# Attention block on one core: projection weights laid out contraction index first by the host

## What is computed

```
x = x + _L0_cond_ref(x, ...); x = x + _L1_cond_ref(x, ...); x = x + _L2_cond_ref(x, ...)
q = jnp.einsum('bsd,ed->bse', x, Wq).reshape(bsz, seqlen, HQ, D)      # 32 heads of 128
k = jnp.einsum('bsd,ed->bse', x, Wk).reshape(bsz, seqlen, HK, D)      # 8 heads of 128
v = jnp.einsum('bsd,ed->bse', x, Wv).reshape(bsz, seqlen, HK, D)
q = _rope(_rmsnorm(q, q_norm_w), pos); k = _rope(_rmsnorm(k, k_norm_w), pos)
...                                                                   # paged cache of keys and values, softmax
return jnp.einsum('bse,de->bsd', o.reshape(bsz, seqlen, HQ * D), Wo)
```

## Time and profile before

| | us |
|---|---|
| median of 3 runs (2461.73 to 2463.17) | 2462.31 |
| the profiled execution | 2460.18 |
| its span, first to last instruction | 2458.0 |
| PE busy | 2359.9 (96%) |
| DVE busy | 1774.6 (72%) |
| ACT busy | 1348.4 (55%) |
| POOL busy | 1152.9 (47%) |
| mean granted TensorE clock, share of full | 0.982 |

### The profile page before, as it was taken

The page is one execution under the profiler, slowest core; times in us unless marked ns, Lnnn a source line. Parts: engine busy times, 40 slices in busy tenths (PEclk is TensorE's granted clock), DMA queues, the critical chain, the costliest instruction groups (busy, mean ns, idle before and its releaser), DMA issues. The chain is left out here.

```text
span 2458.0 us, 51373 instructions
## 1 busy us (share of the span) xinstructions
PE 2359.9 (96%) x15297; PEld 1973.4 (80%) x15297; DVE 1774.6 (72%) x3412; ACT 1348.4 (55%) x2635; POOL 1152.9 (47%) x1362
## 2 busy tenths in 40 slices
PE   6988899999999499999999999999999997999999
PEld 5337777777777399999999999999999997888887
DVE  4656288988889588888888888888888886432221
ACT  6653387788777355555555555555555554321111
POOL 0322134443444277767777777777776774000000
PEclk9999999999999699999999999999999999999999
DMA  9335323333232588888888888888888885743442
GB/s 315 98 102 180 90 80 93 108 108 103 90 107 86 171 274 297 293 292 276 295 288 296 279 287 297 292 289 278 292 295 297 272 293 183 211 126 99 133 137 60
DMA packets 470906, 501.43 MB, mean 204 GB/s; under 512 B 102069, under 2 KB 396981, under 8 KB 466742
## 3 DMA queue, kind: packets, MB, share of 16 engines
q1 hardware_dynamic: 433974, 366.37, 47.2%
q0 software_dynamic: 36864, 134.23, 15.6%
HBM read 404.02 MB, written 96.47 MB: 204 GB/s over the span
## 5 line engine op out<-in xcount | busy, mean ns | idle before, releaser
L1134 POOL TENSOR_TENSOR att_probs<-att_probs,att_inverse 128x512 f32<-128x512 f32 x512 | 536.0, 1047 | 288.6 <-DVE att_inverse L1330 284.0
L1238 ACT ACTIVATE att_probs<-att_probs,att_low 128x544 f32<-128x544 f32 x512 | 383.7, 750 | 515.3 <-DVE att_low L1317 452.0
L1195 PE MATMUL att_o<-att_probs_t,att_values 128*128 128x128 f32 x4096 | 540.9, 275 | 0.0
L1317 DVE CUSTOM_DVE_ANT_0 att_probs<-att_score,att_mask,att_batch_cols 128x544 f32<-128x544 f32 x512 | 400.0, 781 | 138.6 <-PE att_score L1160 99.9
L1195 PEld LDWEIGHTS att_o<-att_probs_t,att_values 128*128 128x128 f32 x4096 | 497.6, 192 | 0.0
L1326 DVE COPY att_probs_t<-att_turn 128x512 f32<-128x512 f32 x512 | 350.7, 685 | 1.2 <-PE att_turn L1175 1.2
L1120 POOL DMA_INDIRECT att_values<-L_cond_v_cache,att_v_rows_of x256 | 282.1, 1102 | 83.1 <-POOL att_v_rows_of L1116 48.8
L1160 PE MATMUL att_score<-att_keys_raw,att_queries_raw 128*128 128x288 f32 (+1 forms) x1024 | 290.7, 407 | 29.5 <-DMA att_queries_raw<-q_t 27.3
L1175 PE MATMUL att_turn<-ident,att_probs 128*128 128x128 f32 x2048 | 311.0, 274 | 1.2 <-POOL att_probs L1134 0.8
L1293 DVE TENSOR_TENSOR att_keys_lo<-att_keys_raw,att_keys_hi 128x384 fp32r<-128x384 f32 (+1 forms) x320 | 259.3, 811 | 17.6 <-ACT att_keys_hi L1231 17.6
L1175 PEld LDWEIGHTS att_turn<-ident,att_probs 128*128 128x128 f32 x2048 | 244.1, 141 | 33.3 <-POOL att_probs L1134 1.4
(11 more groups left out here) (140 smaller groups left out, 4103.1 us busy)
## 6 DMA issues: line engine op xcount, KB each, us to landing
att_keys_raw<-L_cond_k_cache SPq DMA_DIRECT2D x1024, 128.0 KB
q_t<-proj_q_out SPq DMA_DIRECT2D x32, 1024.0 KB, 3.9
att_queries_raw<-q_t SPq DMA_DIRECT2D x64, 512.0 KB
o_t<-att_heads_out SPq DMA_DIRECT2D x64, 512.0 KB, 6.6
out_o_raw<-o_t SPq DMA_DIRECT2D x32, 1024.0 KB, 5.7
prep_natural<-L_cond_weight SPq DMA_DIRECT2D x16, 1024.0 KB, 8.0
w_nat<-L_cond_Wq SPq DMA_DIRECT2D x8, 1024.0 KB, 5.8
v_new<-values_v_out SPq DMA_DIRECT2D x64, 128.0 KB, 2.1
```

What stands on the lines that cost most here:

```text
L1134: nc.gpsimd.tensor_tensor(probs[:, k, 0:L], probs[:, k, 0:L], inverse[:, k:k + 1].to_broadcast([P, L]), ALU.mult).then_inc(probs_ready, 1)
L1195: last = nc.tensor.matmul(o, values[j][:, t, h * D:(h + 1) * D], probs_t[m % 2][:, t * P:(t + 1) * P], start=(t == 0), stop=False, skip_gr ...
L1238: nc.scalar.activation(probs[:, k, :], probs[:, k, :], ACT.Exp, bias=low[k][:, 0:1], scale=-1.0, accum_out=total[k][:, 0:1]).then_inc(exp_ ...
L1317: nc.vector.tensor_tensor_reduce(out=probs[:, k, :], in0=score_ps[:, LEFT:LEFT + KEYS], in1=mask[j][:], scale=batch_cols[j][:, h:h + 1], s ...
```

## The change

The host hands Wv, Wk, Wq and Wo over with the contracted index first (it is not part of the timed program), so a load puts the contracted index on the partitions at once. The transposes of weights go from all three stages. ScalarE and VectorE read the loaded rows in SBUF where they read a bank in PSUM. The waits for `w_turned` become waits for `w_ready` (both halves taken), and ScalarE waits for the load itself. In `projection` the two banks of `proj_w` are gone and `RING` goes from 4 to 5.

```
@@ load_wv
-    sp.dma_start(tile[:], wv.rearrange("(h p) i -> p h i", p=P)[:, heads]).then_inc(loaded, 16)
+    sp.dma_start(tile[:], wv.rearrange("p h c e -> p h (c e)")[:, heads]).then_inc(loaded, 16)
@@ stage_values
+        def wv_rows(h):
+            return w_nat[:, h] if h < WV_EARLY else wv_nat[:, h - WV_EARLY]
...
-            sp.wait_ge(w_turned, WV_EARLY)
+            sp.wait_ge(w_ready, WV_EARLY)
...
-            for h in range(HK):
-                if h == WV_EARLY:
-                    pe.wait_ge(wv_loaded, 16)
-                rows = w_nat[:, h] if h < WV_EARLY else wv_nat[:, h - WV_EARLY]
-                if h >= BANKS:
-                    pe.wait_ge(w_ready, h - BANKS + 1)
-                for c in range(IC):
-                    last = nc.tensor.transpose(w_ps[h % BANKS][:, c * P:(c + 1) * P], rows[:, c * P:(c + 1) * P], ident[:])
-                last.then_inc(w_turned, 1)
             pe.wait_ge(w_ready, HK)
...
             def split_weights(h):
-                act.wait_ge(w_turned, h + 1)
-                nc.scalar.activation(wvt_hi[:, :, h * D:(h + 1) * D], w_ps[h % BANKS].rearrange("p (c e) -> p c e", c=IC),
+                if h == WV_EARLY:
+                    act.wait_ge(wv_loaded, 16)
+                nc.scalar.activation(wvt_hi[:, :, h * D:(h + 1) * D], wv_rows(h).rearrange("p (c e) -> p c e", c=IC),
                                      ACT.Copy).then_inc(wv_hi_ready, 1)
...
-                nc.vector.tensor_tensor(wvt_lo[:, :, cols], w_ps[h % BANKS].rearrange("p (c e) -> p c e", c=IC),
+                nc.vector.tensor_tensor(wvt_lo[:, :, cols], wv_rows(h).rearrange("p (c e) -> p c e", c=IC),
@@ stage_projection
-        RING = 4
+        RING = 5
...
-                    if rc == 1 and not last_head:
-                        turn_weights(h + 1, 1 - u, m)
-
-            for m in range(M):
-                turn_weights(0, 0, m, True)
...
-                act.wait_ge(w_turned, h * M + (m + 1))
-                nc.scalar.activation(w_hi[u][:, m].rearrange("p c e -> p (c e)"), w_ps[(u * M + m) % 2][:],
+                if m == 0 and not first:
+                    act.wait_ge(w_loaded, h * 32)
+                nc.scalar.activation(w_hi[u][:, m].rearrange("p c e -> p (c e)"), w_nat[:, m, :],
...
-                nc.vector.tensor_tensor(w_lo[u][:, m].rearrange("p c e -> p (c e)"), w_ps[(u * M + m) % 2][:],
+                nc.vector.tensor_tensor(w_lo[u][:, m].rearrange("p c e -> p (c e)"), w_nat[:, m, :],
@@ stage_output
-                sp.dma_start(wo_nat[v][:], wo.rearrange("(c p) e -> p c e", p=P)[:, :, h * (REP * D):(h + 1) * (REP * D)]
+                sp.dma_start(wo_raw[v][:], wo[bass.ds(h, 1)].rearrange("h p r o -> p (h r) o")).then_inc(wo_loaded[v], 16)
...
-                sp.wait_ge(turned, (h - 1) * REP)
+                sp.wait_ge(w_ready, (h - 1) * REP)
...
-            turn_weights(0)
             for h in range(HK):
-                if h < HK - 1:
-                    turn_weights(h + 1)
                 pe.wait_ge(w_ready, (h + 1) * REP)
                 products(0, h, True)
@@ LAYOUTS, applied by the host
+    "L3_cond_Wv": lambda a: a.reshape(HK, D, IC, P).transpose(3, 0, 2, 1),
+    "L3_cond_Wk": lambda a: a.reshape(HK, D, IC, P).transpose(0, 3, 2, 1),
+    "L3_cond_Wq": lambda a: a.reshape(HK, REP, D, IC, P).transpose(0, 4, 1, 3, 2),
+    "L3_cond_Wo": lambda a: a.reshape(HID, HK, REP, D).transpose(1, 3, 2, 0),
```

More of the change, by code:

```diff
@@ L469, in stage_values @@
     GC = G // RC
-    BANKS = 4
     with ExitStack() as ctx:
@@ L491, in stage_values @@
         row_f = a_.sb("row_f", [P, 1])
-        w_ps = [a_.ps(f"w{n}") for n in range(BANKS)]
         v_ps = [a_.ps(f"v{u}{n}") for u in range(U) for n in range(2)]
@@ L698, in load_head_weights @@
 def load_head_weights(sp, wq, wk, w_nat, h, loaded):
-    sp.dma_start(w_nat[:, 0, :], wk[bass.ds(h * D, D)]).then_inc(loaded, 16)
-    sp.dma_start(w_nat[:, 1:, :], wq[bass.ds(h * (REP * D), REP * D)].rearrange("(m p) i -> p m i", p=P)).then_inc(loaded, 16)
+    sp.dma_start(w_nat[:, 0, :], wk[bass.ds(h, 1)].rearrange("h p c e -> p (h c e)")).then_inc(loaded, 16)
+    sp.dma_start(w_nat[:, 1:, :], wq[bass.ds(h, 1)].rearrange("h p m c e -> p (h m) (c e)")).then_inc(loaded, 16)
 def stage_projection(nc, wq, wk, ident, x3t_hi, x3t_lo, rope, w_nat, stat, qt_dram, kn_dram):
@@ L727, in stage_projection @@
         stat_t = a_.sb("stat_t", [P, CB, S])
-        w_ps = [a_.ps(f"w{n}") for n in range(2)]
         proj_ps = [a_.ps(f"proj{k}") for k in range(RING)]
@@ L769, in head @@
                 if not last:
-                    sp.wait_ge(w_turned, M)
-                    sp.wait_ge(w_turned, h * M + M)
+                    sp.wait_ge(w_ready, M)
+                    sp.wait_ge(w_ready, h * M + M)
                     load_head_weights(sp, wq, wk, w_nat, h + 1, w_loaded)
@@ L787, in _ @@
         def _(pe):
-            def turn_weights(h, u, m, first=False):
-                if m == 0 and not first:
-                    pe.wait_ge(w_loaded, h * 32)
-                n = (u * M + m) % 2
-                if m >= 2 or not first:
-                    pe.wait_ge(w_ready, h * M + (m - 1))
-                for c in range(IC):
-                    last = nc.tensor.transpose(w_ps[n][:, c * P:(c + 1) * P], w_nat[:, m, c * P:(c + 1) * P], ident[:])
-                last.then_inc(w_turned, 1)
             def sum_k(h, rc):
@@ L843, in _, with split_weights @@
         def _(act):
-            def split_weights(h, u, m):
-                act.wait_ge(w_turned, h * M + (m + 1))
-                nc.scalar.activation(w_hi[u][:, m].rearrange("p c e -> p (c e)"), w_ps[(u * M + m) % 2][:],
+            def split_weights(h, u, m, first=False):
+                if m == 0 and not first:
+                    act.wait_ge(w_loaded, h * 32)
+                nc.scalar.activation(w_hi[u][:, m].rearrange("p c e -> p (c e)"), w_nat[:, m, :],
                                      ACT.Copy).then_inc(w_hi_ready, 1)
@@ L878, in _ @@
             for m in range(M):
-                split_weights(0, 0, m)
+                split_weights(0, 0, m, True)
             heads(act, head)
@@ L1374, in stage_output @@
         a_ = Alloc(nc, ctx, "out")
-        wo_nat = [a_.sb(f"wo_nat{v}", [P, IC, REP * D]) for v in range(2)]
+        wo_raw = [a_.sb(f"wo_raw{v}", [P, REP, HID]) for v in range(2)]
         wot_hi = a_.sb("wot_hi", [P, HQ, HID], F32R)
@@ L1381, in stage_output @@
         y = [a_.sb(f"y_rows{v}", [P, HID]) for v in range(2)]
-        w_ps = [a_.ps(f"w{n}") for n in range(REP)]
         y_ps = [a_.ps(f"y{g}") for g in range(GC)]
         wo_loaded = a_.sem("wo_loaded", 2)
-        turned = a_.sem("turned")
         w_hi_ready = a_.sem("w_hi_ready")
@@ L1462, in _ @@
         def _(pe):
-            def turn_weights(h):
-                pe.wait_ge(wo_loaded[h % 2], 16 * (h // 2) + 16)
-                for r in range(REP):
-                    if h:
-                        pe.wait_ge(w_ready, (h - 1) * REP + (r + 1))
-                    for c in range(IC):
-                        last = nc.tensor.transpose(w_ps[r][:, c * P:(c + 1) * P], wo_nat[h % 2][:, c, r * D:(r + 1) * D], ident[:])
-                    last.then_inc(turned, 1)
             def products(rc, h, first):
@@ L1509, in split_weights @@
             def split_weights(h):
+                act.wait_ge(wo_loaded[h % 2], 16 * (h // 2) + 16)
                 for r in range(REP):
-                    act.wait_ge(turned, h * REP + (r + 1))
-                    nc.scalar.activation(wot_hi[:, h * REP + r, :], w_ps[r][:], ACT.Copy).then_inc(w_hi_ready, 1)
+                    nc.scalar.activation(wot_hi[:, h * REP + r, :], wo_raw[h % 2][:, r, :], ACT.Copy).then_inc(w_hi_ready, 1)
             def split(rc, h, first):
@@ L1571 @@
           "L3_cond_Wo", "L3_cond_q_norm_w", "L3_cond_k_norm_w", "L3_cond_k_cache", "L3_cond_v_cache"]
+LAYOUTS = {
+    "L3_cond_k_cache": lambda a: a.transpose(0, 3, 2, 1),
+    "L3_cond_Wv": lambda a: a.reshape(HK, D, IC, P).transpose(3, 0, 2, 1),
+    "L3_cond_Wk": lambda a: a.reshape(HK, D, IC, P).transpose(0, 3, 2, 1),
+    "L3_cond_Wq": lambda a: a.reshape(HK, REP, D, IC, P).transpose(0, 4, 1, 3, 2),
+    "L3_cond_Wo": lambda a: a.reshape(HID, HK, REP, D).transpose(1, 3, 2, 0),
+}
 def program(nc, ins, freq, out):
@@ L1614 @@
         a = np.asarray(inputs[name])
-        if name == "L3_cond_k_cache":
-            a = a.transpose(0, 3, 2, 1)
+        if name in LAYOUTS:
+            a = LAYOUTS[name](a)
         a = np.ascontiguousarray(a)
```

5 lines of the change are left out of this document (1 added, 4 removed).

## The result

The changed kernel takes 2432.8 us (median, 2431.57 to 2433.2), the kernel before beside it 2462.74 (2461.73 to 2464.03): ratio 0.9877, 95% interval 0.986 to 0.9894, or 29.9 us less. The prediction was 2431.6, the range 2426 to 2440. The profiled execution took 2431.57 us; its span is 2429.4, 28.6 less than that of before.

A forecast was written before the change was run, and what follows sets the result against it. TensorE (busy 96%) was taken to set the pace of projection and output. Terms -16.0 - 4.4 + 0.4 + 1.1 - 1.7 + 0.6 - 10.7 = -30.7 us, from 2462.3 to 2431.6 us; range 2426 to 2440.

The forecast's parts named there:

- Projection, the loop, -16.0: Projection, chunk 1 of seven heads: five turns of weights cost TensorE 2.29 us a head, together -16.0 us.
- Projection, the start, -4.4 and +0.4: Projection's first product comes at 291.9 instead of 296.3, -4.4 us; two more matmuls at the lower clock, +0.4.
- I take 0: Projection's loop: VectorE has 4.7 us free a head, GpSimd's holding takes 0.9 to 2.5, so no time returns.
- a backlog within chunk 1 is covered by the ring: Projection's loop: five result banks let TensorE run four tiles, 11 us, ahead of VectorE's squares; four banks, 8 us.
- Rival (a): Projection: VectorE becomes the bound, held by GpSimd 6.5 us a head against 4.7 free; +12.6 us, 2444; 10%.
- Values, the start, +1.1: Before values' first product, three VectorE subtractions and two GpSimd copies of 0.55 us take turns, +1.1 us.
- can at best make them land sooner: Weight loads: longer runs per partition could only make them land sooner; no size given.
- Output, the start, -1.7: Output's first product comes at 2090.2 instead of 2091.95, the load of o deciding; -1.7 us.
- Output, the clock and the loop, +0.6 and -10.7: Output: 8 matmuls start low instead of 5, +0.6 us; six turns of 1.79 us leave the loop, -10.7.
- (b): Starts of three stages: the lower clock lasts twice as long as taken, +4.8 us, 2436.4; 5%.
- (c): The starts give nothing, because loads and not transposes set them; -25.6 us in all, 2436.7; 5%.
- (d): Output: loads of Wo lengthen the steps, slower than before if a load takes 21 us; 2%.

The follow-up runs named there:

- p_proj: The kernel before, with the change made in projection alone (Wv and Wo as before); 2440.99 us beside 2462.9, ratio 0.9913.
- p_output: The kernel before, with the change made for Wo in output alone; 2450.58 us, ratio 0.9953.

## Why the prediction was right, and where a step of it failed

The mechanism held: in the loops a transpose cost its place in TensorE's queue, at the starts the chain ahead of TensorE decided. By stages the changed kernel is 30.0 us shorter without `maps`, which ended 1.4 us later by chance, where the terms add up to 30.7.

- **Projection, the loop, -16.0.** Chunk 1 and its neighbour took 31.47 us together, as worked out; the products as a whole fell by 15.4, which is 16.0 less the clock. The idle transposes put 15.9 back. Shown.
- **Projection, the start, -4.4 and +0.4.** The start measured -4.3, and 8 to 9 matmuls began low where I took 8.
- **"I take 0": what could fill the place is VectorE.** The sum was right and two steps behind it were wrong. The term "perhaps 0.5 each, 2.5 us" was the upper value; five subtractions measured 2.8 us a head, above it, and with the shorter head 3.0. And "a backlog within chunk 1 is covered by the ring" named the wrong deadline: the banks would have given 8 or 11 us, the sums of query squares give 5.4, of which 1.2 was left at the tightest place and 2.2 behind chunk 1 of most heads. Four banks did as well as five, and two more subtractions cost 10.7 us. The 0 thus came true by a margin that the prediction had not looked at, which is luck. Rival (a) was nearer than its 10%: VectorE does delay TensorE once it has some 1.2 us more to do, but through the sums, which it did not name.
- **Values, the start, +1.1.** +1.35 in the changed kernel, +1.33 alone: close, but only half of it by the mechanism named. The three subtractions grew by 0.67 us where I took 1.1 for them. The other 0.7 is the load of the first 512 rows of x, which landed that much later. This is not chance: from its issue to its landing it takes 7.1 to 7.3 us in the three executions with the old part of values (before, p_proj, p_output) and 7.6 to 7.9 in the eleven with the new one. The load of Wv, issued right behind it, takes 8.4 to 8.6 and 8.9 to 9.2. So "can at best make them land sooner" was wrong here, a term put at nothing (piece 0 of Wo did land sooner, 4.9 us behind its issue where it was 5.8). Whether the new form of Wv's load does it, or the splits that now run beside it, is open. The products took 0.4 more in the changed kernel and 0.9 with this part alone: 10 and 12 matmuls began at the lower clock, 0.2 us each, where it was 8.
- **Output, the start, -1.7.** Measured -1.7, and by the chain described: o_hi starts 8.44 us behind the stage's first issue, when o has landed. The 8.5 that I took for it was a guess between bounds, so that it fits to 0.1 us is luck.
- **Output, the clock and the loop, +0.6 and -10.7.** Together measured -10.0 in the products; nine matmuls began low in place of five, and the steps are 10.88 apart.
- **The other rivals.** (b): 8 to 10 low matmuls at each start, not 16; over all executions, starts without extra products have between none and 14. (c): the starts gave -6.0 together. (d): the longest load of Wo landed in 10.9 us (12.1 before; the median rose from 5.7 to 6.8), against the 16 from which steps would grow.

What stays open is the scatter of `maps`, 178.4 to 182.5 us at its last turn over all these executions, in code that is the same in all. It is as large as most terms of this sum, which is why the sizes above are read within stages, and each kernel has one timeline: the low matmuls at a start scatter by as much as the clock terms.

## What to carry to other kernels

An instruction that leaves the bounding engine's queue is priced by the distance of the same two marks with and without it, and its busy time (41.9 us here, for 28.6) is no price where the engine would have waited anyway. What is moved to another engine's inputs has to be charged there, even when that engine is not the bound: here it took VectorE from 89% to 97% of a head, and the next two subtractions cost 10.7 us. Slack is what is left at the nearest wait of the bounding engine, wherever that is in the program, not in the buffer that one happens to think of and not in a mean over a loop; and when that wait is moved, the next one takes its place. A transfer beside which something changes can land later though nobody touched it: measure it from issue to landing.

## What was unexpected of the hardware

The delay falls on whoever comes second, not on the instruction that was moved. One place in chunk 1 of a head of the changed kernel:

```profile
392.09 0.68 DVE L866 TENSOR_TENSOR proj_w_lo<-w_nat,proj_w_hi 128x512 fp32r<-128x512 f32 x1
392.69 1.78 DVE L879 TENSOR_TENSOR proj_by_cos<-proj_raw,rope 128x512 f32<-128x512 f32 x1
...
392.24 1.68 POOL L949 TENSOR_TENSOR proj_q_out<-proj_by_cos,proj_by_sin 128x512 f32<-128x512 f32 x1 [1.23 <-DVE proj_by_sin L881]
```

The subtraction begins first and takes its 0.68 us. GpSimd's addition, 0.15 us behind it, takes 1.68, where it took 1.29 beside a subtraction from a bank; the multiplication that follows meets the addition and takes 1.78. So the subtractions whose input moved to SBUF stayed at 680 ns on average, and the multiplications went from 860 and 844 to 966 and 903. In the run with idle transposes, the same in all but TensorE's queue, 12 of the 40 subtractions began behind an addition and took 1.5 us each (925 ns on average over the loop), and the multiplications rose less (911 and 870).

TensorE's clock did not follow the extra products alike: nine of them had it at 2.4 GHz at their end in values, ten left it at 1.2 GHz in output, and nine there, in another run with 0.2 us to the first real one, had it at 2.4 GHz from that one on. In values this is more than scatter: in the twelve executions without extra products 8 to 14 matmuls begin low, in the two with them one at most. In output it may be scatter, since in p_proj's execution no matmul began low there without any extra product. What decides is not shown.
